# Target attention over 2048 histories: another order of scores and placing on TensorE, normalisation on GpSimd, weights and targets turned on the host, another warm-up and drain

## The chip, the cores and the metric

The kernel runs on one core of a Trainium2 chip. The time is in device microseconds, from the start of the program to its end. Engines: PE is TensorE (PEld its loading of weights), DVE is VectorE, ACT is ScalarE, POOL is GpSimd, SP is SyncE, which here only issues transfers (SPq in the profile's rows).

## The reference

For each of 2048 targets there is a history of 200 rows of 128 numbers. Scores of four heads of 32 are masked, go through a softmax, and weigh the values. All is float32.

```
q = (target_item @ W_q).reshape(b, H, HD)               # b 2048, H 4, HD 32
k = (history_sequence @ W_k).reshape(b, S, H, HD)       # S 200, D 128
v = (history_sequence @ W_v).reshape(b, S, H, HD)
scores = jnp.einsum('bhd,bshd->bhs', q, k) / SCALE
scores = jnp.where(mask[:, None, :] == 0, NEG, scores)
attn = jax.nn.softmax(scores, axis=-1)
out = jnp.einsum('bhs,bshd->bhd', attn, v).reshape(b, A)
return out @ W_o
```

The kernel never forms k and v. It multiplies W_q with W_k per head beforehand, gives each target a vector per head in the space of the history (u), and scores the raw history with it; the weighted sum of the raw history then goes through the product of W_v and W_o.

## The kernel before, in words

The 2048 targets are done in 64 pairs (`NP`) of two groups of 16; three pairs are a round (`RING` 3, `ROUND` 96 targets). A pair's history is 3.3 MB. SyncE loads it in four quarters: half 0 (12 of 25 rows a partition) of both groups, the next pair's mask, then half 1 (13 rows) of both groups. There are buffers for three pairs (`hist`), and the load of a half waits until the matmuls of `context` of three pairs before have read that half (`ctx_done`).

The work of a pair p, by what it needs:

- VectorE turns the history in blocks of 32x32 (`turn(p, i, half)`, four instructions, L468), since the scores need the feature on the partitions.
- `scores(p, ring, i)` on TensorE (L263): 32 matmuls per group.
- `maximum` on VectorE (L477) adds the mask's bias and takes the max; `exponent` on ScalarE (L392) writes `probs` and their sum.
- `turn_probs` on VectorE: reciprocal of the sum (L486), normalisation `weights = probs * inv_sum` (L488), block turn (L492).
- `place(q)` on TensorE (L277) spreads the probabilities over partitions into `ps_p`; `expand(p)` on ScalarE (L401) writes them with eight instructions into the zero pattern `p_pad`.
- `context(ring, half)` on TensorE (L294): 200 small matmuls of `p_pad` with the raw history.
- `finish` (ACT, L410), `turn_context` (PE, L304), `copy_context` (ACT, L416); once a round `outputs` (PE, L311) and `store` (ACT, L424).

GpSimd prepares `u_pad` from the vectors u (`spread`, L206, 16 small copies a pair, two pairs ahead) and the bias from the mask (`mask_bias`, L210). Once a round TensorE turns the next targets (`transpose_target`, L247) and makes the next u (`combine`, L252), which ScalarE copies (`copy_combined`, L387).

Each engine runs a list in program order, written out by hand, and waits on semaphores. TensorE's list is `step(q, ring, r)`: it places pair q, turns the contexts of pair q-1, does the target turn, the combination or the outputs where the ring says so, then the scores of pair q+1, then the contexts of pair q. Steps 0 and 1 and the last two are unrolled; the others run in a loop of three. VectorE's list interleaves pairs:

```
turn(p, 0, 0); maximum(p-1); turn(p, 1, 0); turn_probs(p-1); turn(p, 0, 1); turn(p, 1, 1)
```

ScalarE's list for pair q is `exponent(q)`, `finish(q-1)`, `expand(q)`, `copy_context(q-1)`, then `copy_target`, `copy_combined` or `store` where the round has one. So an exponential stands behind the expansion and the copies of the pair before.

At the start TensorE turns the three weights and the first targets, makes the products of the weights, and runs 68 transpositions of the identity (`IDLE_TURNS`, L358) before the first scores.

## Time and profile before

| | |
|---|---|
| median of 3 runs | 597.23 us (596.51 to 601.8) |
| the profiled execution | 596.54 us, with a span of 594.7 us in its trace |
| busy share of the span | PE 93%, PEld 75%, DVE 88%, ACT 45%, POOL 52% |
| transfers | 217.58 MB read, 1.05 MB written, mean 369 GB/s |
| TensorE's granted clock over the span | 0.984 of full speed |

The shares are means over a fill, an even part and a drain, which differ much. TensorE is busy nearly always, and so is VectorE; which of them, or which transfer, sets the time must be read from single steps. The page's chain of what ended last lies 81% on PE, 8% on ACT and 4% on DVE.

### The profile page before, as it was taken

How to read it: one execution, taken by the hardware profiler on the slowest of the kernel's cores; microseconds unless marked ns; L12 is line 12 of the kernel's file. 1: busy time of each engine (PE TensorE's matmuls, PEld its weight loads, DVE VectorE, ACT ScalarE, POOL GpSimd, SP SyncE). 2: the span in 40 equal slices, each digit the busy share in tenths (PEclk: the TensorE clock that was granted, in tenths of full speed). 3: DMA queues.
4: the chain of work that ended last, by engine and by line, in shares of the span. 5: the costliest groups of instructions: out<-in, count | busy, mean ns of one | idle time of the engine just before them, and what ended most of it. 6: DMA issues, size and time to landing. Idle time of an engine off the chain costs nothing.

```text
span 594.7 us, 41652 instructions
## 1 busy us (share of the span) xinstructions
PE 551.6 (93%) x18637; PEld 444.7 (75%) x18637; DVE 520.8 (88%) x577; ACT 265.9 (45%) x909; POOL 306.3 (52%) x1123
## 2 busy tenths in 40 slices
PE   5789789999999999999999999999999999999985
PEld 4666567787777878787787877878787777877865
DVE  4576778999999999999999999999999999999960
ACT  2033334554455445544554455445544554455532
POOL 6535353644637465383744737456383654737300
PEclk9978999999999999999999999999999999999998
DMA  8957879999999999999999999999999999999930
GB/s 314 398 178 249 282 279 406 399 400 403 404 408 399 406 406 404 401 402 404 402 406 402 406 401 402 407 400 409 403 403 402 410 398 402 401 406 401 398 134 7
DMA packets 49807, 219.17 MB, mean 369 GB/s; under 512 B 5888, under 2 KB 16656, under 8 KB 49760
## 3 DMA queue, kind: packets, MB, share of 16 engines
q1 hardware_dynamic: 49056, 217.60, 92.9%
q0 software_dynamic: 704, 1.05, 0.5%
q8 instruction: 16, 0.26, 0.2%
q14 instruction: 31, 0.25, 0.1%
HBM read 217.58 MB, written 1.05 MB: 368 GB/s over the span
## 4 chain that ended last, share of the span: by engine, by line
PE 81%; ACT 8%; issue 5%; DVE 4%; DMA 1%; SPq 1%; POOLq 0%; POOL 0%; DVEq 0%
PE ps_c L294 30%; PE ps_s L263 28%; PE ps_p L277 11%; ACT p_pad L401 8%; PE ps_y L304 4%; PE ps_u L252 3%; PE ps_u L311 3%; DVE blocks L468 3%; PE ps_p L358 2%; DMA w_in<-L_rec_W_o 1%; DVE probs_t L492 1%; DVE weights L488 1%; SPq L149 0%; SPq L158 0%; SPq L143 0%
## 5 line engine op out<-in xcount | busy, mean ns | idle before, releaser
L468 DVE STREAM_TRANSPOSE blocks<-hist 128x1536 f32<-128x1536 f32 (+1 forms) x256 | 455.7, 1814 | 9.0 <-DMA hist<-r_history_sequence 8.7
L206 POOL COPY u_pad<-u_sb 32x32 f32<-32x32 f32 x1024 | 234.2, 229 | 196.2 <-ACT u_sb L387 138.2
L263 PE MATMUL ps_s<-blocks,u_pad 128*32 128x200 f32 x4096 | 198.9, 342 | 14.8 <-ACT p_pad L401 9.7
L294 PE MATMUL ps_c<-hist,p_pad 64*32 64x128 f32 x12800 | 202.2, 272 | 8.7 <-issue 6.5
L294 PEld LDWEIGHTS ps_c<-hist,p_pad 64*32 64x32 f32 x12800 | 183.5, 106 | 30.5 <-issue 28.2
L401 ACT ACTIVATE p_pad<-ps_p,own 128x200 f32<-128x200 f32 x512 | 170.2, 444 | 42.9 <-PE ps_p L277 42.9
L263 PEld LDWEIGHTS ps_s<-blocks,u_pad 128*32 128x32 f32 x4096 | 125.7, 111 | 71.8 <-DVE blocks L468 25.6
L410 ACT COPY ctx_sb<-ps_c 128x128 f32<-128x128 f32 x128 | 27.8, 269 | 139.7 <-PE ps_c L294 139.7
L210 POOL TENSOR_SCALAR bias<-mask 128x200 f32<-128x200 int32 x64 | 56.4, 882 | 61.2 <-DVE neg_max L477 56.7
L392 ACT ACTIVATE probs<-neg_score,neg_max 128x200 f32<-128x200 f32 x64 | 29.6, 463 | 125.9 <-DVE neg_max L477 125.9
L277 PE MATMUL ps_p<-probs_t,place_sel 128*64 128x112 f32 x1024 | 64.0, 267 | 7.9 <-DVE probs_t L492 5.4
L277 PEld LDWEIGHTS ps_p<-probs_t,place_sel 128*64 128x64 f32 x1024 | 50.2, 138 | 24.6 <-DVE probs_t L492 16.5
L477 DVE CUSTOM_DVE_ANT_0 neg_score<-ps_s,bias 128x200 f32<-128x200 f32 x64 | 23.5, 367 | 37.2 <-PE ps_s L263 37.0
L304 PE MATMUL ps_y<-par_sel,ctx_sb 128*128 128x64 f32 x256 | 42.6, 289 | 0.0
L304 PEld LDWEIGHTS ps_y<-par_sel,ctx_sb 128*128 128x128 f32 x256 | 33.8, 192 | 9.2 <-issue 0.3
L492 DVE STREAM_TRANSPOSE probs_t<-weights 128x224 f32<-128x224 f32 x64 | 26.3, 411 | 2.8 <-DVE weights L488 0.2
L416 ACT COPY ctx_t<-ps_y 128x128 f32<-128x128 f32 x64 | 28.0, 437 | 0.1
L252 PE MATMUL ps_u<-x_t,w_qk 128*128 128x96 f32 x176 | 24.8, 286 | 0.9 <-ACT w_qk L430 0.9
L311 PE MATMUL ps_u<-w_vo,ctx_t 128*96 128x128 f32 x176 | 23.5, 277 | 0.5 <-ACT ctx_t L416 0.5
L488 DVE TENSOR_SCALAR weights<-probs,inv_sum 128x200 f32<-128x200 f32 x64 | 21.5, 336 | 2.3
L252 PEld LDWEIGHTS ps_u<-x_t,w_qk 128*128 128x128 f32 x176 | 22.2, 198 | 1.3 <-ACT w_qk L430 1.1
L311 PEld LDWEIGHTS ps_u<-w_vo,ctx_t 128*96 128x96 f32 x176 | 19.9, 163 | 0.8 <-ACT ctx_t L416 0.6
(42 smaller groups left out, 110.4 us busy)
## 6 DMA issues: line engine op xcount, KB each, us to landing
hist<-r_history_sequence SPq DMA_DIRECT2D x128, 832.0 KB, 8.1
hist<-r_history_sequence SPq DMA_DIRECT2D x128, 768.0 KB, 5.8
mask<-r_mask SPq DMA_DIRECT2D x64, 100.0 KB, 6.0
x_sb<-r_target_item SPq DMA_DIRECT2D x21, 48.0 KB, 8.5
out<-out_sb POOLq DMA_DIRECT2D x21, 48.0 KB, 4.7
w_in<-L_rec_W_q SPq DMA_DIRECT2D x1, 64.0 KB, 1.9
w_in<-L_rec_W_k SPq DMA_DIRECT2D x1, 64.0 KB, 2.0
w_in<-L_rec_W_v SPq DMA_DIRECT2D x1, 64.0 KB, 4.5
```

The costliest lines, as they stand in the source:

```text
L206: pool.tensor_copy(to, source[Q * c:Q * c + Q, a]).then_inc(u_pad_ready, 1)
L210: pool.tensor_scalar(bias[p % 2][:, :], mask_sb[p % RING][:, :], 0.0, BIG, ALU.is_equal, ALU.mult).then_inc(bias_ready, 1)
L252: mm = pe.matmul(ps_u[:, h * ROUND:(h + 1) * ROUND], w_qk[:, h, :], x_t[:, :], start=True, stop=True)
L263: mm = pe.matmul(ps_s[ring][Q * b:Q * b + Q, 0:S].rearrange("p (t j) -> p t j", j=J), u_pad[ring][:, i, b, c, :], blocks[slot][:, :, c, J ...
L277: mm = pe.matmul(ps_p[64 * alpha:64 * alpha + 64, 0:4 * TQ * 16].rearrange("p (q x i r) -> p x q i r", q=TQ, x=4, i=2)[:, x], place_sel[:, ...
L294: mm = pe.matmul(ps_c[alpha][at:at + Q, 0:D], p_pad[ring][rows, t + par, i, :], hist[2 * ring + i][rows, t + par, :], start=(t == 0), stop ...
L304: mm = pe.matmul(ps_y[:, 64 * alpha:64 * alpha + 64], ctx_sb[:, alpha, :], par_sel[:, :, :].rearrange("p i r -> p (i r)"), start=True, sto ...
L311: mm = pe.matmul(ps_u[0:ROUND, H * ROUND:H * ROUND + D], ctx_t[:, h, :], w_vo[:, h, :], start=(h == 0), stop=(h == H - 1))
L392: act.activation(probs[p % 2][:, :], neg_score[p % 2][:, :], ACT.Exp, bias=neg_max[:, 0:1], scale=-1.0, accum_out=row_sum[p % 2][:, 0:1]). ...
L401: op = act.activation(p_pad[p % RING][:, :, :, H * k:H * k + H].rearrange("p t i h -> p (t i) h"), source[:, k // 4], ACT.Copy, scale=own[ ...
L468: dve.transpose(blocks[g % BLOCKS][:, t0:t1].rearrange("p t c k -> p (t c k)"), hist[g % SLOTS][:, t0:t1, :].rearrange("p t d -> p (t d)") ...
L492: dve.transpose(probs_t[:, :, :].rearrange("p q r -> p (q r)"), weights[:, :]).then_inc(probs_turned, 1)
```

## The change

What it does, part by part:

- TensorE's `step` begins with half of the scores of pair q+1, then places pair q, then does the other half; then the turn of the contexts and the combination or the outputs; then it waits for the expansion and does one transposition of the identity, then the contexts.
- VectorE no longer normalises. It makes the reciprocal after its second turn, then does a third turn, then turns the probabilities. GpSimd normalises (`normalise`), ahead of the spreading of the pair two further on.
- `p_pad` is one buffer instead of three.
- Weights W_q, W_k, W_v and the targets come transposed from the host, ahead of the launch. The turns on TensorE, their copies on ScalarE, and the loads of targets once a round go; the rest of the targets comes in one transfer of 1 MB behind pair 1's history. ScalarE issues four of the small loads at the start.
- The warm-up is 50 matmuls of 32 columns. One step is unrolled ahead of the loop instead of two; two steps are unrolled behind it, and the last is written out, with 12 transpositions ahead of its contexts and the outputs between the two halves. `outputs` also runs in the first round, on zeros.

The core of the diff:

```diff
@@ pool @@
+            def normalise(p):
+                pool.wait_ge(inv_ready, p + 1)
+                wait(pool, probs_turned, p)
+                pool.tensor_scalar(weights[:, 0:S], probs[p % 2][:, :], inv_sum[:, 0:1], None,
+                                   ALU.mult).then_inc(weighted, 1)
...
             for p in range(NP):
+                pool.wait_ge(bias_ready, min(p + 2, NP))
+                normalise(p)
+                pool.wait_ge(weighted, p + 1)
                 if p + 2 < NP:
-                    pool.wait_ge(bias_ready, p + 2)
                     spread(p + 2)
@@ tensor @@
-            def step(q, ring, r, first=False, ahead=True, targets=True):
+            def step(q, ring, r, first=False):
 
+                scores(q + 1, (ring + 1) % RING, 0)
                 place(q)
+                scores(q + 1, (ring + 1) % RING, 1)
                 if not first:
                     pe.wait_ge(ctx_copied, 2 * q)
                     turn_context()
-                if targets and (ring == 2 or first):
-                    transpose_target(r + 2 if ring == 2 else 1)
-                if targets and ring == 0 and not first:
-                    combine(r + 1)
-                if ring == 1 and not (isinstance(r, int) and r == 0):
-                    outputs(q - 1)
-                if ahead:
-                    scores(q + 1, (ring + 1) % RING, 0)
-                    pe.wait_ge(expanded, q + 1)
-                    scores(q + 1, (ring + 1) % RING, 1)
-                else:
-                    pe.wait_ge(expanded, q + 1)
+                    if ring == 0:
+                        combine(r + 1)
+                    if ring == 1:
+                        outputs(q - 1)
+
+                pe.wait_ge(expanded, q + 1)
+                pe.transpose(ps_p[:, 0:P], ident[:, :], ident[:, :])
                 context(ring, 0)
                 context(ring, 1)
                 if first:
+                    pe.wait_ge(rest_loaded, 16)
+                    pe.wait_ge(x_zero, 1)
                     combine(1)
...
-            for _ in range(IDLE_TURNS):
-                pe.transpose(ps_p[:, 0:P], ident[:, :], ident[:, :])
-            for i in range(2):
-                scores(0, 0, i)
+            for _ in range(IDLE):
+                pe.matmul(ps_p[0:Q, 0:Q], ident[:, 0:Q], ident[:, 0:Q], start=True, stop=True)
+            scores(0, 0, 0)
+            scores(0, 0, 1)
             step(0, 0, 0, first=True)
-            step(1, 1, 0)
             with pe.Fori(0, LOOPS) as r:
+                step(3 * r + 1, 1, r)
                 step(3 * r + 2, 2, r)
                 step(3 * r + 3, 0, r + 1)
-                step(3 * r + 4, 1, r + 1)
-            step(NP - 2, 2, NR - 2, targets=False)
-            step(NP - 1, 0, NR - 1, ahead=False, targets=False)
+            step(NP - 3, 1, NR - 2)
+            step(NP - 2, 2, NR - 2)
+
+            place(NP - 1)
+            pe.wait_ge(ctx_copied, 2 * (NP - 1))
+            turn_context()
+            for _ in range(WARM):
+                pe.transpose(ps_s[1][:, 0:P], ident[:, :], ident[:, :])
+            pe.wait_ge(expanded, NP)
+            context(0, 0)
             outputs(NP - 1)
+            context(0, 1)
@@ scalar @@
-                wait(act, ctx_done, 2 * (p - RING) + 2)
+                wait(act, ctx_done, 2 * p)
...
+            store(NR - 2)
             finish(NP - 1)
-            store(NR - 2)
@@ vector @@
+            def reciprocal(p):
                 dve.wait_ge(exp_done, p + 1)
-                if p == 0:
-                    dve.wait_ge(weights_zero, 1)
-                wait(dve, probs_turned, p)
+                wait(dve, weighted, p)
                 dve.reciprocal(inv_sum[:, :], row_sum[p % 2][:, :]).then_inc(inv_ready, 1)
-                dve.wait_ge(inv_ready, p + 1)
-                dve.tensor_scalar(weights[:, 0:S], probs[p % 2][:, :], inv_sum[:, 0:1], None,
-                                  ALU.mult).then_inc(weighted, 1)
```

How it moves the instructions. On TensorE, in the loop, the step with the outputs (`scores` L263, `place` L277, `turn_context` L304, `outputs` L311, `context` L294), before:

```order
L273 REGISTER_ALU
L277 MATMUL ps_p<-probs_t,place_sel 64x7x16 x8
L319 REGISTER_ALU
L304 MATMUL ps_y<-par_sel,ctx_sb 128x64 x2
L311 MATMUL ps_u<-w_vo,ctx_t 96x128 x4
L257 ISA
L259 ISA
L263 MATMUL ps_s<-blocks,u_pad 32x200 x16
```

And after (the same functions now stand at L256, L270, L297, L304 and L287; L322 is the transposition):

```order
L256 MATMUL ps_s<-blocks,u_pad 32x200 x16
L130 REGISTER_ALU
L270 MATMUL ps_p<-probs_t,place_sel 64x7x16 x8
L250 REGISTER_ALU
L256 MATMUL ps_s<-blocks,u_pad 32x200 x16
L314 REGISTER_ALU
L297 MATMUL ps_y<-par_sel,ctx_sb 128x64 x2
L304 MATMUL ps_u<-w_vo,ctx_t 96x128 x4
L322 MATMUL ps_p<-ident 128x128
L287 MATMUL ps_c<-hist,p_pad 32x128 x100
```

Half of the scores moved ahead of the placing; both halves moved ahead of the context's turn and the outputs, which now stand between the scores and the contexts.

On VectorE, one pair in the even part, from the max on (`turn` L468, reciprocal L486, normalisation L488, turn of the probabilities L492), before:

```order
L477 ISA neg_score,neg_max<-ps_s,bias 128x200
L477 ISA neg_max 128x1
L468 STREAM_TRANSPOSE blocks<-hist 128x1536
L486 RECIPROCAL inv_sum<-row_sum 128x1
L488 TENSOR_SCALAR weights<-probs,inv_sum 128x200
L492 STREAM_TRANSPOSE probs_t<-weights 128x224
L468 STREAM_TRANSPOSE blocks<-hist 128x1664 x2
```

And after (now L467, L458, L474 and L479):

```order
L467 ISA neg_score,neg_max<-ps_s,bias 128x200
L467 ISA neg_max 128x1
L458 STREAM_TRANSPOSE blocks<-hist 128x1536
L474 RECIPROCAL inv_sum<-row_sum 128x1
L458 STREAM_TRANSPOSE blocks<-hist 128x1664
L479 STREAM_TRANSPOSE probs_t<-weights 128x224
L458 STREAM_TRANSPOSE blocks<-hist 128x1664
```

The third block turn moved between the reciprocal and the turn of the probabilities, and the normalisation left the engine.

On SyncE, the first transfers, before (`w_in` weights, `x_sb` and `x_t` targets):

```order
L143 DMA w_in<-L_rec_W_q 128x128
L143 DMA w_in<-L_rec_W_k 128x128
L144 DMA x_sb<-r_target_item 96x128
L158 DMA hist<-r_history_sequence 128x1536 x2
L149 DMA mask<-r_mask 128x1x200 x2
L167 DMA w_in<-L_rec_W_v 128x128
```

And after, as far as the transfer of the remaining targets:

```order
L137 DMA w_in<-L_rec_W_q 128x128
L151 DMA hist<-r_history_sequence 128x1536 x2
L142 DMA mask<-r_mask 128x1x200 x2
L151 DMA hist<-r_history_sequence 128x1664 x2
L151 DMA hist<-r_history_sequence 128x1536 x2
L142 DMA mask<-r_mask 128x1x200
L151 DMA hist<-r_history_sequence 128x1664 x2
L159 DMA x_t<-r_target_item 128x1952
```

The history moved ahead of all but one of the small loads, and the remaining targets stand ahead of pair 2's history.

## Rows read from the trace of the kernel before

**Rows 1.** Windows, even part: span; busy us (count) by engine; clock, DMA share, GB/s.

```profile
92.80:575.20 482.40, 468.48 (x16521) 378.68 (x16516) 461.06 (x513) 232.75 (x797) 260.39 (x955) 1.00 1.00 399
```

**Rows 2.** Timeline of a step: start us, us, engine, line, operation, count, idle before.

```profile
304.32 2.84 PEld L294 LDWEIGHTS ps_c<-hist,p_pad 64*32 64x32 f32 x200 [0.32 <-issue]
...
305.96 0.80 SPq L158 DMA_DIRECT2D hist<-r_history_sequence  x2
...
307.44 0.99 PE L277 MATMUL ps_p<-probs_t,place_sel 128*64 128x112 f32 x16
...
308.35 0.66 PE L304 MATMUL ps_y<-par_sel,ctx_sb 128*128 128x64 f32 x4
308.47 2.66 ACT L401 ACTIVATE p_pad<-ps_p,own 128x200 f32<-128x200 f32 x8 [0.57 <-PE ps_p L277]
...
308.85 1.07 PE L311 MATMUL ps_u<-w_vo,ctx_t 128*96 128x128 f32 x8
...
309.84 2.98 PE L263 MATMUL ps_s<-blocks,u_pad 128*32 128x200 f32 x64
310.97 0.43 ACT L416 COPY ctx_t<-ps_y 128x128 f32<-128x128 f32 x1
311.13 0.36 ACT L424 COPY out_sb<-ps_u 96x128 f32<-96x128 f32 x1
311.25 1.18 PEld L263 LDWEIGHTS ps_s<-blocks,u_pad 128*32 128x32 f32 x32 [0.24 <-DVE blocks L468]
...
312.88 0.37 DVE L477 CUSTOM_DVE_ANT_0 neg_score<-ps_s,bias 128x200 f32<-128x200 f32 x1 [0.26 <-PE ps_s L263]
...
313.29 0.46 ACT L392 ACTIVATE probs<-neg_score,neg_max 128x200 f32<-128x200 f32 x1 [1.80 <-DVE neg_max L477]
...
314.87 0.12 DVE L486 RECIPROCAL inv_sum<-row_sum 128x1 f32<-128x1 f32 x1
...
315.03 0.33 DVE L488 TENSOR_SCALAR weights<-probs,inv_sum 128x200 f32<-128x200 f32 x1
```

**Rows 3.** Timeline: ScalarE's copy of the combination, in the step with `combine`.

```profile
302.70 0.59 ACT L387 COPY u_sb<-ps_u 128x384 f32<-128x384 f32 x1
```

**Rows 4.** Single loads issued at 94.3, 102.7, 104.2, 305.96, 9.83: us to landing last.

```profile
hist<-r_history_sequence SPq DMA_DIRECT2D x1, 768.0 KB, 4.1
...
hist<-r_history_sequence SPq DMA_DIRECT2D x1, 768.0 KB, 4.3
...
hist<-r_history_sequence SPq DMA_DIRECT2D x1, 832.0 KB, 7.1
...
hist<-r_history_sequence SPq DMA_DIRECT2D x1, 768.0 KB, 4.6
...
hist<-r_history_sequence SPq DMA_DIRECT2D x1, 768.0 KB, 15.9
```

**Rows 5.** Groups by line and form, whole span: busy us, mean ns, idle before.

```profile
L468 DVE STREAM_TRANSPOSE blocks<-hist 128x1664 f32<-128x1664 f32 x128 | 234.6, 1870 | 1.6 <-DMA hist<-r_history_sequence 1.6
...
L210 POOL TENSOR_SCALAR bias<-mask 128x200 f32<-128x200 int32 x64 | 56.4, 882 | 61.2 <-DVE neg_max L477 56.7 <-PE ps_s L263 1.0
```

**Rows 6.** Timeline: the max of pairs 0, 2 and 6.

```profile
24.82 0.37 DVE L477 CUSTOM_DVE_ANT_0 neg_score<-ps_s,bias 128x200 f32<-128x200 f32 x1 [7.09 <-PE ps_s L263]
...
48.02 0.37 DVE L477 CUSTOM_DVE_ANT_0 neg_score<-ps_s,bias 128x200 f32<-128x200 f32 x1 [2.51 <-PE ps_s L263]
...
92.77 0.37 DVE L477 CUSTOM_DVE_ANT_0 neg_score<-ps_s,bias 128x200 f32<-128x200 f32 x1 [0.79 <-PE ps_s L263]
```

**Rows 7.** Windows of the warm-up alone: PE and PEld busy (count), clock, DMA, GB/s.

```profile
12.30:16.30 4.00, 4.00 (x19) 4.00 (x20) 1.00 1.02 399
16.50:21.70 5.20, 5.20 (x50) 5.17 (x48) 1.00 1.02 414
```

**Rows 8.** Timeline of the drain: contexts of pair 62 (end) and pair 63.

```profile
578.93 0.64 PE L294 MATMUL ps_c<-hist,p_pad 64*32 64x128 f32 x17 [1.06 <-issue]
...
583.24 4.64 PE L294 MATMUL ps_c<-hist,p_pad 64*32 64x128 f32 x200 [2.17 <-ACT p_pad L401]
```

105 lines of the change are left out of this document (43 added, 62 removed).

## The prediction

> **What bounds the kernel now.** I read the windows by stage first, then the timeline of one step, then the loads. The window from 92.8 us, where the max of pair 6 stands [rows 6], to 575.2 is even running with the array's clock at 1.00 [rows 1]; ahead of it lies the fill, behind it the drain. It holds 513 instructions of VectorE, nine a step, so 57 steps: 482.4 / 57 = 8.46 us each. What one step costs decides nearly everything, since 0.1 us of it is 5.7 us.
>
> Within a step TensorE is full. Counted from the start of the placing matmuls at 307.44 [rows 2]: placing 0.91, the turn of the contexts 0.50, the outputs 0.99, the first half of the scores 1.41, the second 1.50, the contexts 3.12 (304.32 to 307.44). These add up to 8.43. VectorE is nearly full as well: its wait before the max is 0.26 us. ScalarE is not: it expands the probabilities from 308.47, copies the outputs, and then waits 1.80 us for the max before the exponential [rows 2]. The transfers run at 399 GB/s with their engines busy all the time [rows 1], yet no block turn waits for one in the even part: a load that is issued 1.64 us into the contexts (305.96 against 304.32) lands 4.6 us later, and other such loads 4.1 to 4.3 [rows 4], just before its turn.
>
> **The even part.** Four edits meet here.
>
> VectorE loses the normalisation, 0.36 us with its gap, the 0.33 us row of 315.03. GpSimd takes it. Nothing shows this form there. The nearest row is the mask's operation on the same 128x200, 0.88 us [rows 5]; its floor is VectorE's 0.33. I take 0.88, as it is the same engine. The cover is a block turn of 1.87 us [rows 5], so 0.88 and two handovers are hidden; with that cover gone it would cost 1.0 us a step. On GpSimd the spreading and the mask wait behind it. In the even part GpSimd is busy 260.39 / 57 = 4.6 us a step [rows 1], so there is room for 0.88 more. VectorE's saving is worth nothing unless VectorE ends last.
>
> TensorE loses one target turn in three steps and gains one small transposition in each. The transpositions of the warm-up took 5.2 us for 50 at the full clock, 0.10 us each [rows 7]. In the order after, a step is 1.41 + 0.91 + 1.50 + 0.50 + 0.99 + 0.10 + 3.12 = 8.53 us where there are outputs or a combination (two steps in three). In the third, the expansion ends last: it starts 1.03 us after placing, lasts 2.66, and 0.12 passes until TensorE starts, so 3.81 + 0.10 + 3.12 + 1.41 = 8.44. The mean is 8.50: TensorE's own order gains nothing, because it was full before. What the moved order does remove is the wait of the scores' second half for the expansion.
>
> The moved order costs ScalarE its slack. Before, from placing to the end of the scores there were 5.31 us, which hid the expansion and two copies. Now there are 0.91 + 1.50 = 2.41, so the slack of 1.80 turns into a delay of 1.1 us. In the step with outputs these end 3.90 us after placing starts; the copy of the context starts at 4.00, the store at 4.16 and lasts 0.36, the exponential starts at 4.52, and the reciprocal 0.61 later at 5.13 (0.46 for the exponential, an estimate of 0.15 for reading its sum and the handover), the block turn at 5.29 and ends at 7.16; half the scores start at 7.21 and the next placing 1.41 later, at 8.62. With the copy of 0.59 us [rows 3] for the combination it is 8.69. With 8.44 for the third step the mean is **8.58 us**.
>
> The loads then decide. The contexts, which free the history buffers, no longer follow the scores at once: they start 0.91 + 1.50 + 0.50 + 0.99 + 0.10 = 4.00 us after placing (3.91 in the third step), though the turns on VectorE keep their place against the max. Taking 3.97, the first quarter of the pair three further on is issued at 5.61 and lands at 9.91, 4.3 us later. The third quarter lands 4.3 us behind it (issues at 102.70 and 104.19, landing after 4.3 and 7.1 us [rows 4]), at 14.21. Its turn takes 1.87, the handover 0.05, half the scores 1.41: 17.54 us to a placing that is two steps on, so 8.77 a step. With the shortest latency, 4.1 us [rows 4], it is 8.67. The stream itself sets no such limit: 414 GB/s in [rows 7] would allow 8.2 us for a pair's 3.4 MB. I take **8.73**, nearer to 8.77 because the quiet 4.1 came once, right after a stall. Against 8.46 that is +0.27 x 57 = **+15.4 us**. The bounds are 8.44 and 8.85, which are -1 and +22 us.
>
> The page "DMA: Bandwidth & Descriptors" of the Trainium skill, in "Anatomy of one DMA", gives 2.0 us and the bytes over 436 GB/s for a transfer from GpSimd's queue, which as an estimate is 3.8 us for a quarter. The trace has 4.3 for SyncE's queue, and the trace decides. By the page the loads would chain at about 8.5 us, and the engines' 8.58 would rule, which is the first rival.
>
> **The fill.** The weights and targets come turned from the host, so two turns with their copies go, and the weights for the output are no longer loaded behind the history. The warm-up of 68 transpositions, 12.3 to 21.7 us [rows 7], becomes 50 matmuls of 32 columns, at most 5 us by the 0.10 of a full transposition. Then the loads decide. VectorE had done the turns that stand ahead of the first max at 24.82 - 7.09 = 17.7 [rows 6]. SyncE now issues two small loads fewer ahead of the history, at 0.4 us each (0.80 for two in [rows 2]), so these turns end at 16.9, and with them stands the first max, instead of at 24.82. The next max must let the first turn of pair 2 pass, whose load, issued at 9.83, landed 15.9 us later at 25.7 [rows 4]. It is 0.8 earlier, but the rest of the targets, now 1 MB in one transfer ahead of it, costs 2.4 us at 414 GB/s. So turn at 27.3 for 1.8, and max 1 at 29.1. The combination behind the first contexts still holds the second exponential; I add 1.2 to a step of 8.7 for it: max 2 at 39.0 against 48.02, 9 us ahead.
>
> From there to max 6 the kernel before took 44.75 us for four steps whose code runs for the first time, 11.2 us a step, with gaps like the first of [rows 8]. After, the loop is entered one step earlier, so one such step becomes even: 11.7 + 11.7 + 9.7 + 8.7 = 41.8, and max 6 stands at 80.8 against 92.77: **-11.9 us**. The two full cold steps are taken at a little over the mean of 11.2, the two others below it, since the last of the four was already half even. Bounds: -6, if small matmuls don't raise the clock, and -15.
>
> **The drain.** Two unrolled steps follow the loop and then a part of a third, so one more cold step: +1.1, the idle time ahead of the first of [rows 8]. The contexts of pair 62 start 1.5 us later. The last contexts ran at half clock, 4.64 us [rows 8]; with the transpositions ahead of them 3.12 are possible, -1.5. The outputs go between the two halves, +0.9, and the store ahead no longer holds the last, -0.5. The sum is **+1.5**, bounds 0 and +4.
>
> The page "TensorE: Matmul & The Clock Gate" of the Trainium skill says in "PE-mode transpose" that transpositions don't count as activity for the clock. Here they do: 19 records in the first 4.0 us and then 50 in 5.2 [rows 7]. By the page the -1.5 would go, and the time would be 1.5 us longer, which is within the range.
>
> **The sum.** 594.7 + 15.4 - 11.9 + 1.5 = 599.7 us of span. The profiled execution took 596.54 with a span of 594.7, so 1.84 lie around it, and it stands 0.7 below the median of 597.23. That gives 601.5, or 602.2 against the median; I say **602**.
>
> **Rivals.** *The loads land in time.* Latency falls below 4.1 us once the stream is no longer full, and the engines' 8.58 decides: +7 instead of +15, 593 us. For it: 4.1 was seen. Against it: both latencies were taken where the queue had drained. Chance 0.2.
>
> *The step stays or shrinks.* Then the fill alone shows. The contexts are entered with 0.32 us idle on TensorE's loads [rows 2]; if the small transposition swallows that, and ScalarE's copies overlap more than I count, the step is 8.40 to 8.46, and the time 583 to 587. Against it: the chain over the exponential has no such idle time in it. Chance 0.15.
>
> *The loads chain worse (slower than before).* After a disturbance the first quarter took 4.6 us [rows 4] and the queue caught up only slowly. Now each late landing delays two steps on, and nothing catches up. At 8.83 the time is 608; it passes +1% (603.2) from 8.75 us a step. Speaking for it: the sum by the usual 4.3 is already 8.77. Chance 0.3.
>
> *It doesn't hide the normalisation.* GpSimd takes far longer than 0.88, above 1.6 us, and each step gains the difference. The spreading copies run beside the same turns without lengthening them, so I give it 0.03, 610 us and more.
>
> **How the numbers follow.** The forecast, 8.66 to 8.75 a step with its fill, has 0.32. A step of 0.1 us either way is 6 us and the fill may be off by 4, so within each case some chance passes the 1% bounds, 591.3 and 603.2; 1% is about what a measurement of this kernel can tell from no change. Faster: 0.15, half of the first rival's 0.2, and 0.02 of the forecast, 0.27. Slower: most of the 0.3, the 0.03 and 0.05 of the forecast, 0.34. Same: 0.39. The range 583 to 611 leaves out 0.05 below and 0.08 above.
>
> **What the next profile should show.** The distance of two maxes in the even part, 8.6 to 8.8 us; idle time of the reciprocal on VectorE, ended by ScalarE's exponential; block turns that wait for history loads, in many steps; ScalarE without its wait for the max; transfers at some 390 GB/s; first max near 17, the seventh near 81. I am wrong if the turns never wait for loads and the step is under 8.5, or if the fill ends where it did.

## The result, and the profile after

The changed kernel takes 624.08 us (median of 4 runs, 622.41 to 627.03), the kernel before 597.11 beside it: a ratio of 1.044, 95% interval 1.040 to 1.048. It is slower, by more than the range of 583 to 611 allowed. The profiled execution has a span of 623.4 us.

The profile's page of the changed kernel, its line of busy time and three of its groups (busy us, mean ns, then the idle time just before them and what ended it):

```profile
PE 557.1 (89%) x18727; PEld 444.7 (71%) x18727; DVE 504.5 (81%) x513; ACT 260.6 (42%) x885; POOL 357.1 (57%) x1189
...
L458 DVE STREAM_TRANSPOSE blocks<-hist 128x1536 f32<-128x1536 f32 (+1 forms) x256 | 469.7, 1836 | 70.1 <-DMA hist<-r_history_sequence 68.9
...
L206 POOL TENSOR_SCALAR weights<-probs,inv_sum 128x200 f32<-128x200 f32 x64 | 50.7, 791 | 179.2 <-issue 169.8
...
L387 ACT ACTIVATE probs<-neg_score,neg_max 128x200 f32<-128x200 f32 x64 | 30.6, 479 | 8.0 <-DVE neg_max L467 8.0
```

VectorE's block turns now wait 68.9 us in all for the history. Between 100 and 550 us alone they wait 47.4 us in 82 times; in the kernel before it was 0.5 us in 3 times. GpSimd's normalising takes 0.79 us, a little under the 0.88 taken for it. ScalarE, which waited 1.80 us a step for the max [rows 2], waits for it once in the whole run, 8.0 us at the start: its slack is gone, as forecast.

The windows of the changed kernel, from the max of pair 6 to 0.7 us before that of pair 63, and the fill before (us, busy time with the number of instructions of PE, PEld, DVE, ACT, POOL, granted clock, DMA share, GB/s):

```profile
85.70:602.20 516.50, 478.84 (x16541) 383.70 (x16545) 446.94 (x455) 228.19 (x778) 309.54 (x1029) 1.00 0.96 371
...
18.16:85.70 67.54, 53.02 (x1534) 39.96 (x1535) 47.19 (x49) 21.93 (x74) 33.65 (x114) 0.90 0.84 311
```

From max to max the 57 steps take 602.88 - 85.70 = 517.2 us instead of the 482.4 of [rows 1], and the transfers run at 371 instead of 399 GB/s: they wait too. TensorE is busy for 93% of this stretch, 97% before; VectorE for 87%, 96% before. Four maxes, from the timeline of VectorE (start, us): of pairs 2, 6, 62 and 63.

```profile
42.84 0.37 DVE L467 CUSTOM_DVE_ANT_0 neg_score<-ps_s,bias 128x200 f32<-128x200 f32 x1 [2.00 <-PE ps_s L256]
...
85.70 0.37 DVE L467 CUSTOM_DVE_ANT_0 neg_score<-ps_s,bias 128x200 f32<-128x200 f32 x1 [0.25 <-POOL bias L200]
...
590.78 0.33 DVE L467 CUSTOM_DVE_ANT_0 neg_score<-ps_s,bias 128x200 f32<-128x200 f32 x1
...
602.88 0.37 DVE L467 CUSTOM_DVE_ANT_0 neg_score<-ps_s,bias 128x200 f32<-128x200 f32 x1 [4.56 <-PE ps_s L256]
```

Fifty-six even steps in 590.78 - 85.70 = 505.08 us are **9.02 us** each; before, the same 56 took 566.85 - 92.77 = 474.08 us, 8.47 each. The last step is 12.1 instead of 8.3. The bill, against 594.7: the 56 even steps +31.0; the last, cold step +3.8; pair 6 at 85.70 instead of 92.77, -7.1; the drain behind the last max 20.5 instead of 19.5, +1.0; the sum is 623.4, the span that was found.

Now one round of the chain of the loads, from the changed kernel's timeline (start, us, engine, what, and the idle time before it): placing, contexts, the issue of the load, the turns that wait for it, the scores, the next placings.

```profile
298.60 0.99 PE L270 MATMUL ps_p<-probs_t,place_sel 128*64 128x112 f32 x16
...
302.61 3.10 PE L287 MATMUL ps_c<-hist,p_pad 64*32 64x128 f32 x200
...
304.25 0.80 SPq L151 DMA_DIRECT2D hist<-r_history_sequence  x2
...
307.42 0.99 PE L270 MATMUL ps_p<-probs_t,place_sel 128*64 128x112 f32 x16
...
308.67 1.78 DVE L458 STREAM_TRANSPOSE blocks<-hist 128x1536 f32<-128x1536 f32 x1 [0.71 <-DMA hist<-r_history_sequence]
...
311.44 3.10 PE L287 MATMUL ps_c<-hist,p_pad 64*32 64x128 f32 x200
...
312.87 1.91 DVE L458 STREAM_TRANSPOSE blocks<-hist 128x1664 f32<-128x1664 f32 x1 [0.30 <-DMA hist<-r_history_sequence]
...
314.92 1.56 PE L256 MATMUL ps_s<-blocks,u_pad 128*32 128x200 f32 x32 [0.37 <-DVE blocks L458]
...
316.41 0.99 PE L270 MATMUL ps_p<-probs_t,place_sel 128*64 128x112 f32 x16
317.73 1.78 DVE L458 STREAM_TRANSPOSE blocks<-hist 128x1536 f32<-128x1536 f32 x1 [0.86 <-DMA hist<-r_history_sequence]
...
321.94 1.91 DVE L458 STREAM_TRANSPOSE blocks<-hist 128x1664 f32<-128x1664 f32 x1 [0.32 <-DMA hist<-r_history_sequence]
...
323.99 1.56 PE L256 MATMUL ps_s<-blocks,u_pad 128*32 128x200 f32 x32 [0.47 <-DVE blocks L458]
325.48 0.99 PE L270 MATMUL ps_p<-probs_t,place_sel 128*64 128x112 f32 x16
```

From 298.60 to 316.41 two steps pass: 4.01 to the contexts, 1.64 to the issue, 4.42 until the quarter has landed and its turn starts, 4.20 to the third quarter's turn, 2.05 to the scores, 1.49 to the placing: 17.81. From 307.42 to 325.48 it is 18.06, with 4.65 for the landing. The forecast had 17.54 with the same links. In 40 such rounds between 100 and 550 us, the landing took 4.1 to 5.5 us, 4.5 in the mean.

The same chain was there before, but with room in it. The load issued at 305.96 landed after 4.6 us [rows 4], at 310.56; its turn is the last of the three that the timeline of the kernel before counts together here, and began near 310.9:

```profile
307.30 5.32 DVE L468 STREAM_TRANSPOSE blocks<-hist 128x1664 f32<-128x1664 f32 x3
```

The contexts then started 0.1 us ahead of the max (312.75 against 312.88). Now they start 1.0 to 1.2 us behind it (302.61, 311.44 and 320.42 against 301.37, 310.37 and 319.43), and the 0.3 us of room are gone.

In one place the profile misleads. It puts 27 waits of the scores between 100 and 550 us, 15.0 us in all, down to GpSimd's `u_pad`. But the copies that go on then are for a pair further on. The scores start 0.14 us behind the end of the third turn in the three rounds from 303.88 on, so it is the turn that they wait for.

### The profile page after: what moved, and what is told of

It is laid out like the page before. It is cut to its first block, busy times and chain, and to the rows that moved or that the text cites. A ratio compares the mean times of both kernels' runs of the same rounds, so it can differ in the third digit from the quotient of the medians.

```text
span 623.4 us, 41775 instructions
## 1 busy us (share of the span) xinstructions
PE 557.1 (89%) x18727; PEld 444.7 (71%) x18727; DVE 504.5 (81%) x513; ACT 260.6 (42%) x885; POOL 357.1 (57%) x1189
## 4 chain that ended last, share of the span: by engine, by line
PE 49%; issue 23%; POOL 14%; DMA 7%; ACT 3%; DVE 3%; SPq 1%; POOLq 0%; DVEq 0%; ACTq 0%
PE ps_s L256 26%; PE ps_c L287 10%; PE ps_p L270 8%; POOL u_pad L196 8%; DMA hist<-r_history_sequence 7%; POOL weights L206 5%; ACT p_pad L396 3%; DVE blocks L458 2%; PE ps_u L304 2%; PE ps_y L297 2%; PE ps_u L244 1%; SPq L151 1%; PE ps_p L322 1%; DVE neg_score L467 1%; POOL bias L200 0%
## 5 line engine op out<-in xcount | busy, mean ns | idle before, releaser
L458 DVE STREAM_TRANSPOSE blocks<-hist 128x1536 f32<-128x1536 f32 (+1 forms) x256 | 469.7, 1836 | 70.1 <-DMA hist<-r_history_sequence 68.9
L256 PE MATMUL ps_s<-blocks,u_pad 128*32 128x200 f32 x4096 | 204.0, 340 | 32.0 <-POOL u_pad L196 18.3
L287 PE MATMUL ps_c<-hist,p_pad 64*32 64x128 f32 x12800 | 202.0, 271 | 7.7 <-issue 6.8
L287 PEld LDWEIGHTS ps_c<-hist,p_pad 64*32 64x32 f32 x12800 | 182.7, 105 | 17.9 <-issue 8.8
L256 PEld LDWEIGHTS ps_s<-blocks,u_pad 128*32 128x32 f32 x4096 | 123.9, 111 | 88.0 <-POOL u_pad L196 42.1
L206 POOL TENSOR_SCALAR weights<-probs,inv_sum 128x200 f32<-128x200 f32 x64 | 50.7, 791 | 179.2 <-issue 169.8
L270 PEld LDWEIGHTS ps_p<-probs_t,place_sel 128*64 128x64 f32 x1024 | 51.4, 140 | 21.2 <-issue 21.2
L270 PE MATMUL ps_p<-probs_t,place_sel 128*64 128x112 f32 x1024 | 65.4, 272 | 0.0
L297 PEld LDWEIGHTS ps_y<-par_sel,ctx_sb 128*128 128x128 f32 x256 | 33.4, 190 | 20.7 <-issue 19.7
L297 PE MATMUL ps_y<-par_sel,ctx_sb 128*128 128x64 f32 x256 | 42.1, 287 | 0.5 <-ACT ctx_sb L405 0.5
L467 DVE CUSTOM_DVE_ANT_0 neg_score<-ps_s,bias 128x200 f32<-128x200 f32 x64 | 21.8, 341 | 15.4 <-PE ps_s L256 14.3
L322 PE MATMUL ps_p<-ident 128*128 128x128 f32 x63 | 18.4, 292 | 15.2 <-ACT p_pad L396 15.2
L244 PE MATMUL ps_u<-x_t,w_qk 128*128 (+1 forms) x176 | 24.8, 286 | 2.5 <-DMA x_t<-r_target_item 2.5
L304 PE MATMUL ps_u<-w_vo,ctx_t 128*96 128x128 f32 x184 | 24.6, 277 | 0.5 <-ACT ctx_t L411 0.5
L479 DVE STREAM_TRANSPOSE probs_t<-weights 128x224 f32<-128x224 f32 x64 | 23.7, 370 | 1.0 <-POOL weights L206 1.0
```

The lines of the kernel that those rows point to most:

```text
L206: pool.tensor_scalar(weights[:, 0:S], probs[p % 2][:, :], inv_sum[:, 0:1], None, ALU.mult).then_inc(weighted, 1)
L244: mm = pe.matmul(ps_u[:, h * ROUND:(h + 1) * ROUND], w_qk[:, h, :], x_t[:, bass.ds(at, ROUND)] if not isinstance(r, int) else x_t[:, at:at ...
L256: mm = pe.matmul(ps_s[ring][Q * b:Q * b + Q, 0:S].rearrange("p (t j) -> p t j", j=J), u_pad[ring][:, i, b, c, :], blocks[slot][:, :, c, J ...
L270: mm = pe.matmul(ps_p[64 * alpha:64 * alpha + 64, 0:4 * TQ * 16].rearrange("p (q x i r) -> p x q i r", q=TQ, x=4, i=2)[:, x], place_sel[:, ...
L287: mm = pe.matmul(ps_c[alpha][at:at + Q, 0:D], p_pad[rows, t + par, i, :], hist[2 * ring + i][rows, t + par, :], start=(t == 0), stop=(t + ...
L297: mm = pe.matmul(ps_y[:, 64 * alpha:64 * alpha + 64], ctx_sb[:, alpha, :], par_sel[:, :, :].rearrange("p i r -> p (i r)"), start=True, sto ...
```

## The experiments

"Even step" is the distance of the maxes of pairs 9 and 60, by 51; the kernel before has 8.47 by it, the changed one 9.02. Ratios are to the kernel before, timed beside.

| run | us | ratio, 95% interval | even step |
|---|---|---|---|
| e1_step_order_back | 665.53 | 1.114 (1.108 to 1.120) | 9.74 |
| e2_step_order_alone | 649.71 | 1.086 (1.081 to 1.090) | 9.30 |
| e3_gpsimd_normalises_alone | 671.89 | 1.122 (1.117 to 1.127) | 9.77 |
| e4_short_loads | 596.08 | single run | 8.65 |
| e5_fill_and_drain_alone | 593.00 | 0.991 (0.987 to 0.995) | 8.46 |
| e6_before_short_loads | 592.87 | single run | 8.48 |
| e7_step_order_alone_short_loads | 639.62 | single run | 9.25 |
| e8_placing_first | 622.07 | 1.039 (1.030 to 1.048) | 9.00 |
| e9_two_unrolled_steps | 754.89 | single run | long stalls |
| e10_exponential_before_copy | 747.56 | 1.249 (1.243 to 1.256) | long stalls |
| e11_no_normalising | 626.59 | single run | 9.04 |
| e12_no_holding_transpositions | 626.50 | single run | 9.03 |
| e13_one_unrolled_exponential_first | 591.84 | 0.989 (0.984 to 0.994) | 8.54 |
| e14_two_unrolled_shifted | 913.25 | single run | long stalls |
| e15_two_unrolled_shifted_exponential_first | 898.60 | 1.502 (1.495 to 1.510) | long stalls |
| e16_changed_exponential_first | 624.57 | single run | 9.00 |
| e17_two_unrolled_back | 591.25 | 0.986 (0.982 to 0.991) | 8.47 |
| e18_changed_shifted | 772.42 | single run | long stalls |

### The two edits of the even step, each alone

**e1**: the changed kernel, TensorE's order as before.

```diff
-                scores(q + 1, (ring + 1) % RING, 0)
                 place(q)
-                scores(q + 1, (ring + 1) % RING, 1)
 ...
+                scores(q + 1, (ring + 1) % RING, 0)
                 pe.wait_ge(expanded, q + 1)
-                pe.transpose(ps_p[:, 0:P], ident[:, :], ident[:, :])
+                scores(q + 1, (ring + 1) % RING, 1)
```

> The changed kernel with TensorE's order of a step as before (placing, turn of contexts, combination or outputs, both halves of the scores with the wait for the expansion between them, contexts, no small transposition); all else stays changed: GpSimd normalises behind the third block turn, new fill and drain. Theory A (late contexts free the history buffers late, and the loads chain over two steps): contexts follow the scores again, the loads are back in time, the even step falls from 9.02 to 8.40-8.45 us, and with the fill's gain the time is 587-592 us. Rival B (the third block turn and GpSimd's normalisation lengthen the way to the placing): the step stays at 8.8-9.1, 610-625 us. Rival C (the stream of loads is slower whatever the order, some 375 GB/s): the same 615-625 us.

All three theories failed: 665.5 us, slower than the whole change. Rival B had the cause, a longer way to the placing, but not its size. The timeline of TensorE and VectorE in a step of e1:

```profile
303.66 1.89 DVE L456 STREAM_TRANSPOSE blocks<-hist 128x1664 f32<-128x1664 f32 x1
...
305.47 0.37 DVE L477 STREAM_TRANSPOSE probs_t<-weights 128x224 f32<-128x224 f32 x1
...
305.98 0.99 PE L270 MATMUL ps_p<-probs_t,place_sel 128*64 128x112 f32 x16 [1.38 <-DVE probs_t L477]
...
311.42 0.37 DVE L465 CUSTOM_DVE_ANT_0 neg_score<-ps_s,bias 128x200 f32<-128x200 f32 x1 [2.04 <-PE ps_s L256]
```

The probabilities' turn now stands behind the third block turn, and the old order of TensorE places first of all. So TensorE stands for 1.38 us at the placing, and VectorE then stands 2.04 for the scores. The turns hardly wait for loads: between 100 and 550 us, 4.3 us in 11 times.

**e2**: the kernel before with TensorE's new order alone. **e3**: the kernel before with GpSimd's normalising and the third turn ahead of the probabilities' turn alone.

> The kernel before with the new order of a step on TensorE alone (half the scores, placing, the other half, turn of contexts, target turn, combination or outputs, wait for the expansion, one small transposition, contexts). VectorE normalises as before, three p_pad buffers, old fill and drain. Theory A: the even step is 8.9-9.1 us as in the changed kernel, the time 624-634 us. Rival B: without GpSimd's normalisation the step is 8.5-8.65 us, 600-608 us.

> The kernel before with GpSimd's normalisation behind the third block turn alone; TensorE's order, fill and drain as before. Theory A: TensorE was full at 8.43 us a step and still is, so the step is 8.40-8.50 and the time 594-600 us. Placing moves 1.8 us against the max, so a gain is possible only where VectorE ended last. Rival B: the later placing makes the expansion late, the step grows to 9 us, 620-630 us.

e2, with 649.7 us and 9.30 a step, came out above both of its cases. e3, with 671.9, is far from the 594 to 600 of its theory and above its rival's 620 to 630 too: its even step is that of e1 (9.77 and 9.74), with the same kind of wait, 1.29 us at a placing. So neither edit is good by itself. +8.6% and +12.2% alone, they are +4.4% together: the new order puts half of the scores, which needs the third turn, ahead of the placing, and GpSimd's normalising lets the third turn come first.

### What the loads cost

**e4** is the changed kernel with short loads, **e6** the kernel before with them, **e7** is e2 with them. From pair 3 on each load brings only 6 of its 12 or 13 rows a partition:

```diff
+                        t9 = t1 if p < RING else t0 + 6
-                            hist[g % SLOTS][:, t0:t1, :], history_v[g * P:(g + 1) * P, t0:t1, :],
+                            hist[g % SLOTS][:, t0:t9, :], history_v[g * P:(g + 1) * P, t0:t9, :],
```

> The changed kernel, but from pair 3 on every load of history brings only 6 of the 12 or 13 rows a partition (old rows stay in the buffers, so the output differs from the reference's); all waits on the buffers stay. Theory A: a load lands about 1 us earlier and the third quarter 3 us earlier, so the loads stop binding and the engines' own chain shows, 8.6-8.75 us a step, 600-607 us. Rival B (GpSimd or ScalarE set the step): unchanged at 9.02, 622-626 us.

> The kernel before, with each load from pair 3 on cut to 6 rows of its half (the rest of the slot keeps old data, so the output is not the reference's); VectorE, TensorE and all waits stay. Control for the short loads of the changed kernel. Theory A (before, the loads are not what ends a step): even step within 0.05 of 8.46 us, 594 to 598. Rival B (short loads speed up any version, by less traffic): even step 8.2 us or less, under 585.

> TensorE's new step order alone (the 650 us run) with each load from pair 3 on cut to 6 rows, so not the reference's output. Theory A (late contexts bind this version through the loads, and VectorE's normalising ahead of the third turn adds its 0.9 us only in that chain): even step 8.6 to 8.8, 605 to 620. Rival B (the normalising itself sets the step, since the first half of the scores waits for the third turn): even step 9.1 or more, 635 or more.

The list of waits, of e4 and then of e7 (us in total, times, longest):

```profile
DVE neg_score L468 <- PE ps_s L257: 34.3, 60, 3.8
DVE inv_sum L475 <- ACT probs L388: 22.0, 42, 4.6
DVE blocks L459 <- DMA hist<-r_history_sequence: 16.3, 26, 4.3
```

```profile
DVE neg_score L478 <- PE ps_s L264: 59.1, 64, 8.0
...
DVE inv_sum L487 <- ACT probs L393: 21.9, 42, 4.4
...
DVE blocks L469 <- DMA hist<-r_history_sequence: 7.7, 6, 5.2
```

Before, short loads leave the even step as it was (8.48 against 8.47): the loads bound nothing in it. (Its 592.9 us are below the 594 of its theory, by a shorter fill: pair 6 at 87.83.) In the changed kernel they take it from 9.02 to 8.65. So of the 0.55 us lost a step the loads hold 0.37, and the engines' own chain 0.18; in e4 the reciprocal waits for ScalarE's exponential in 42 of the steps, and the max for the scores, as the forecast had it. The time, 596.1 us, is below the 600 of its theory, since the fill became shorter too (pair 6 at 79.05). e7 met its rival: with the loads out of the way the new order alone still takes 9.25, so there it is VectorE's normalising and the probabilities' turn, 0.9 us ahead of the third turn, that count. From 9.25 (e7) to 8.65 (e4), GpSimd's edit is worth some 0.6 us a step under the new order with short loads; with full loads, where they bind, it is 0.28 (9.30 in e2 to 9.02). Both pairs of kernels differ in fill, drain and `p_pad` as well; e5 below, which has these and the old even step, takes 8.46.

**e8** places ahead of both halves of the scores in the changed kernel.

> The changed kernel with placing moved ahead of the first half of the next scores, nothing else. Theory A (late contexts bind through the loads; placing comes 0.9 us and the contexts some 0.5 us sooner): no wait for loads over 0.3 us, even step 8.6 to 8.8, 600 to 612. Rival B (TensorE now stands still at the placing until the probabilities are turned, which VectorE does behind its third block turn, and the half of the scores that covered this comes later): even step 9.1 to 9.6, 630 to 655.

It is 622 us, no better and no worse than the changed kernel, between its two theories. From the timeline of TensorE in e8:

```profile
306.12 3.10 PE L287 MATMUL ps_c<-hist,p_pad 64*32 64x128 f32 x200
310.67 0.99 PE L270 MATMUL ps_p<-probs_t,place_sel 128*64 128x112 f32 x16 [1.44 <-DVE probs_t L479]
```

TensorE waits 1.44 us here for the probabilities' turn, 54 us in all, and the turns still wait 64 us for loads, against 69. The placing moved ahead of the half of the scores, but it now waits for that turn, so it hardly came sooner.

**e11** leaves GpSimd's normalising out and keeps its waits and signals.

> The changed kernel with GpSimd's normalising (0.79 us each) shortened to the write of one unused number, with all its waits and signals; the weights stay zero, so the output is not the reference's. Theory A (GpSimd's work lies beside the third turn and no chain of the step runs over it; loads and TensorE's order set 9.02 us): even step 8.95 to 9.02, 619 to 624. Rival B (GpSimd's 0.8 us or its share of VectorE's access stands in the step's chain): even step 8.7 or less, under 608.

An even step of 9.04, a little above its theory's 9.02: the 0.79 us on GpSimd is hidden. That rival is out. The third turn takes 1.91 us here as well, so it isn't GpSimd's normalising that lengthens it from the 1.87 of [rows 5].

### The drain and the fill

**e12**: `WARM = 12` becomes 0.

> The changed kernel without the 12 transpositions of the drain. Theory A (they keep TensorE's clock up over its wait for the last expansion): the granted clock falls after the last placing and the last two context halves and outputs (4.9 us of work) take 2 to 4 us more, drain 22.5 to 24.5 us. Rival B (the clock would have stayed up, and 1.48 us of transpositions lay in a wait of 2.3 us anyway): drain 20.5 us within 0.3.

The end of e12, TensorE's timeline and two windows (columns as above):

```profile
610.51 0.66 PE L297 MATMUL ps_y<-par_sel,ctx_sb 128*128 128x64 f32 x4
613.33 1.59 PE L287 MATMUL ps_c<-hist,p_pad 64*32 64x128 f32 x96 [2.17 <-ACT p_pad L396]
```

```profile
610.00:615.00 5.00, 2.83 (x114) 2.35 (x110) 0.00 (x0) 3.06 (x10) 0.00 (x0) 1.00 0.02 3
615.00:620.00 5.00, 3.76 (x117) 2.94 (x118) 0.00 (x0) 1.07 (x4) 0.54 (x1) 1.00 0.05 13
```

After 2.17 us of idle time, without any transposition, the clock is still 1.00 and the 96 records take the same 1.59 us. From the last max to the end it is 20.4 us, with the transpositions 20.5. The transpositions changed nothing here. In the kernel before the last contexts came behind the same 2.17 us of wait, yet they took 4.64 us [rows 8], and from 583.24 to 586.00 us the granted clock was 0.50. What sets this difference, no run shows.

**e5** keeps the fill, the drain and the turned weights, and undoes both edits of the even step; **e13** adds to it this edit of ScalarE's list, and **e16** makes the same edit in the changed kernel:

```diff
                 exponent(q)
+                r = q // RING
+                if q % RING == 1 and r + 1 < NR:
+                    copy_combined(r + 1)
 ...
-                if q % RING == 0 and r + 1 < NR:
-                    copy_combined(r + 1)
```

> The changed kernel with both steady edits undone: TensorE's steps in the order of the kernel before (placing, contexts' turn, outputs, first half of the next scores, second half, contexts), VectorE normalising ahead of the third block turn. What is left of the change is the fill, the drain and the weights and targets handed over transposed. Theory A (both steady edits are the loss, the fill is worth what it showed): even step 8.46 us as before, pair 6's maximum at 82 to 86 us, drain 0.5 to 1.5 us longer; 587 to 592 us. Rival B (an earlier start only uses up loads that are then missing, and the even step pays it back): 595 to 599.

> The 593 us version (fill and drain of the change, steady steps as before, one unrolled step ahead of the loop) with ScalarE's copy of the next round's combined queries behind the next pair's exponential. Theory A (the copy held pair 1's exponential, and so its placing, in the fill; the loop keeps its place in the code and has no long stalls): pair 2's maximum at 38 to 40.5 us instead of 42.56, even step 8.46, no TensorE stall over 0.4 us in the loop, 588 to 592 us. Rival B (loads or cold steps take the gain back by pair 6): pair 6 within 0.5 us of 85.90, 592 to 594.

> The changed kernel with ScalarE's copy of the combined queries behind the next pair's exponential, nothing else. Tests the term of the fill. Theory A (pair 2's maximum came at 42.84 instead of the forecast 39.0 since pair 1's exponential stood behind that copy until 34.5, and GpSimd's spread of pair 2 behind its normalising): pair 2's maximum at 36.5 to 39.5, even step unchanged within 0.06 of 9.02, 618 to 623. Rival B (the half-speed clock and cold code set it): pair 2's maximum later than 41.5.

e5's theory holds for the steps: pair 6 at 85.90, then 8.46 a step, last step 10.8 (8.3 before), span 589.6. Its median of 593.0 is 1.0 above the range, and 0.5 to 1.4% faster than the kernel before. So the fill keeps its gain, and nearly all of the loss is in the even step. Now the fill of the changed kernel, timelines of ScalarE, VectorE and TensorE:

```profile
34.14 0.48 ACT L382 COPY u_sb<-ps_u 128x384 f32<-128x384 f32 x1 [4.51 <-PE ps_u L244]
34.52 0.46 ACT L387 ACTIVATE probs<-neg_score,neg_max 128x200 f32<-128x200 f32 x1
```

```profile
35.10 0.16 DVE L474 RECIPROCAL inv_sum<-row_sum 128x1 f32<-128x1 f32 x1 [4.17 <-ACT probs L387]
35.18 1.91 DVE L458 STREAM_TRANSPOSE blocks<-hist 128x1664 f32<-128x1664 f32 x1
```

```profile
37.23 2.30 PE L256 MATMUL ps_s<-blocks,u_pad 128*32 128x200 f32 x32 [3.13 <-DVE blocks L458]
39.46 1.76 PE L270 MATMUL ps_p<-probs_t,place_sel 128*64 128x112 f32 x16
```

The exponential of pair 1, whose max was ready at 29.2, stands behind the copy of the next round's vectors until 34.52. VectorE's list is in order, so the third turn of pair 2 waits behind the reciprocal of pair 1, which waits 4.17 us for that exponential, and TensorE stands 3.13 us for the turn. The half of the scores and the placing behind it run at a lower clock: 2.30 and 1.76 us instead of 1.56 and 0.99, with 0.73 granted from 37 to 39 us and 0.50 from 39 to 41.

With the copy behind the exponential (e16), pair 2's max comes at 39.39 instead of 42.84, as the forecast had it (39.0). But pair 6 stands at 86.58, no sooner, and the time stays at 624.6. The four steps between take it back: TensorE stands still with nothing to wait for 7.5 us in all instead of 4.6, in stalls of up to 2.4 us, and the turns wait 10.9 us for loads instead of 5.6. In e13 pair 2 gains only 0.6, far from its theory's 38 to 40.5, and pair 6 1.3.

How much of this hangs on the loads, e4 and e6 show. With short loads the four steps from pair 2 to pair 6 take 36.3 us instead of 42.9 in the changed kernel, and 38.8 instead of 44.8 in the kernel before. Some of that is turns that wait less for history; some is TensorE's stalls, 1.3 us instead of 4.6 in e4. Why these become shorter, no run separates.

### Where the loop lies in the code

**e9** is e5 with step 1 unrolled again ahead of the loop and one step fewer behind it; **e10** is e9 with ScalarE's edit.

```diff
+            step(1, 1, 0)
             with pe.Fori(0, LOOPS) as r:
-                step(3 * r + 1, 1, r)
                 step(3 * r + 2, 2, r)
                 step(3 * r + 3, 0, r + 1)
-            step(NP - 3, 1, NR - 2)
+                step(3 * r + 4, 1, r + 1)
             step(NP - 2, 2, NR - 2)
```

> The 593 us version (fill and drain of the change, steady steps as before) with step 1 unrolled again ahead of the loop and only one unrolled step behind it, so the layout of the kernel before: what 'one unrolled step' alone is worth. Theory A (the unrolled step is cold wherever it stands, so the change moved its stalls from the fill to the end): pair 6's maximum 1 to 2 us later than 85.90, the last step 2.5 us shorter (8.4 instead of 10.84), span 587.5 to 589.5. Rival B (a cold step costs more in the fill, where the half-speed clock stands in it too): pair 6 at 88.5 or later, span 590 to 593.

> The same as the run with two unrolled steps, and on ScalarE the copy of the combined queries of the next round moved behind the next pair's exponential. Theory A (in the fill, pair 1's exponential stood 5.2 us behind that copy, which waits for pair 0's contexts and the combination; placing of pair 1 then waits only for TensorE's own work): pair 2's maximum 1.5 to 2.5 us sooner than 42.56, all else equal, median 588 to 591, ratio to before 0.985 to 0.990. Rival B (TensorE's own row of contexts, combination, placing and cold scores sets pair 2's maximum, or loads do a pair later): pair 6 within 0.5 us of the run with two unrolled steps, 591 to 594.

No theory had 750 us. From TensorE's timeline in e9, and its row of the instruction queue (packets, MB, share), with that of the changed kernel behind it:

```profile
104.67 3.10 PE L279 MATMUL ps_c<-hist,p_pad 64*32 64x128 f32 x200
115.13 1.76 PE L262 MATMUL ps_p<-probs_t,place_sel 128*64 128x112 f32 x16 [7.35 <-issue]
```

```profile
q8 instruction: 98, 1.61, 0.9%
```

```profile
q8 instruction: 17, 0.28, 0.2%
```

TensorE stands for 7.35 us with nothing to wait for, at the loop's start, then 0.83 and 2.10 us in the same pass; and the instruction queue brings 98 packets of code of 16.4 KB, where the whole code is 17. So the loop of three steps is loaded again as it runs. Behind the long stall the granted clock is 0.50 from 115.1 to 117.0 us (placing in 1.76). Four runs tried whether this follows the place of the loop. Their only edit is the number of short matmuls in the warm-up: `IDLE` 64 instead of 50 in e9 and e10 (**e14**, **e15**), 32 in e10 (**e17**), 68 in the changed kernel (**e18**).

> The 755 us version (two unrolled steps ahead of the loop) with 64 instead of 50 short matmuls in the warm-up, which moves everything behind them 14 matmuls later in TensorE's code; nothing else differs. Theory A (the stalls of some 8 us at each pass of the loop are code that is loaded again, and whether it is depends on where the loop's first and last instructions lie in the code): no stalls over 0.5 us in the loop, instruction queue some 17 packets instead of 98, even step 8.46, 588 to 594. Rival B (it is the loop that begins with step 2 instead of step 1, wherever it lies): 750 to 760 again.

> The same shift and ScalarE's copy behind the exponential, two unrolled steps ahead of the loop. Theory A (as in the two runs beside it, their gains add): 586 to 590, and 1 to 2 us under the version with one unrolled step. Rival B (the loop's layout still costs its repeated loads): 740 to 760.

> Two unrolled steps ahead of the loop, ScalarE's copy behind the exponential, and 32 instead of 50 matmuls in the warm-up: everything behind moves 18 matmuls forward in TensorE's code. The even steps are those of the 593 us version. Theory A (repeated loads of code depend on where the loop lies; 14 matmuls backward made them 188 instead of 98, so 18 forward bring them down): some 17 packets in the instruction queue, even step 8.46, last step 8.4 to 8.6, 586 to 592 us. Rival B (two unrolled steps ahead of the loop are bad at any place): over 640 us.

> The changed kernel with 68 instead of 50 matmuls in the warm-up, nothing else: 1.7 us more of warm-up, and everything behind it 18 matmuls later in TensorE's code. Theory A (place in the code decides, in the changed kernel too): instruction queue 60 packets or more instead of 17, over 700 us. Rival B (the changed kernel's loop, which begins with step 1, is safe at any place): 17 packets, 623 to 627.

The rows of the instruction queue of e14, of e17 and of e18:

```profile
q8 instruction: 188, 3.08, 1.5%
```

```profile
q8 instruction: 17, 0.28, 0.2%
```

```profile
q8 instruction: 98, 1.61, 0.9%
```

e14 and e15 went the wrong way for their theories' times and for their rivals' alike, 913 and 899 us. It is a matter of place all the same: matmuls that stand ahead of the loop in TensorE's code are 238 in the changed kernel and e5 (17 packets), 256 in e18 (98), 366 in e17 (17), 384 in e9 (98), 398 in e14 (188). Some 1,090 matmuls in 280 KB are 0.257 KB each, as an estimate, so the two cases with 98 packets, 128 matmuls apart, differ by just two packets of 16.4 KB: the loop starts at the same offset in one. The long stalls fit the packets. e9 and e18 have nine stalls of over 5 us, one at every second pass of the loop's 20; e14 has 19, one at each jump back; and 81 and 171 packets beyond the 17 are nine for each of them. Eighteen matmuls of warm-up, 1.2 us of work, cost the changed kernel 148 us. Why one offset reloads and another doesn't is left open.

The page "Runtime: NRT & Kernel Launch" of the Trainium skill, in "Instruction fetch mechanics", gives TensorE 128 KiB of instruction memory, filled in blocks of 16 KiB; the size of a packet agrees. It also warns that a taken branch out of two blocks stops for a fetch. The changed kernel's loop, 434 matmuls or some 111 KB by the estimate above, jumps back at each of its passes without one: its 17 packets are the whole code.

e17 also tells what one unrolled step is worth. Its pair 6 stands at 89.49, its last step takes 8.3; in e13 it is 84.60 and 11.2. So the unrolled step costs 4.9 us ahead of the loop and 2.9 behind it, by one profile each and with the shorter warm-up counted in. In the medians, 591.25 and 591.84, no difference shows. The ratios of e5, e13 and e17, 0.991, 0.989 and 0.986, have intervals that overlap: which of the three is best isn't shown.

## Why the prediction was wrong

**The even step: mechanism right, size wrong.** The forecast named all that the profile shows: the contexts 4.0 us after placing, block turns that wait for loads in most steps, ScalarE without its wait, the normalising hidden on GpSimd. e4 confirms both layers, the engines' chain (8.58 forecast, 8.65 found) and the loads over it. The step that failed is the sum of the loads' chain, 17.54 us and "I take 8.73". Found were 17.81 and 18.06 in two rounds, and 9.02 a step. The landing took 4.42 and 4.65 instead of 4.3 (4.5 in the mean of 40 rounds), the third turn 1.91 instead of 1.87, the handover 0.14 instead of 0.05, the half of the scores with its switch to placing 1.49 instead of 1.41, the contexts' start 4.01 instead of 3.97; only the distance of the third quarter was shorter, 4.20 instead of 4.3. Each is small, and nearly all have one sign. On top of that the 8.77 of the sum was taken down to 8.73 for a 4.1 us load seen once, though [rows 4] had a 4.6 as well. From 8.73 to 9.02 over 56 steps is 16 us, two thirds of the miss of 23.7 in the span. The rival "loads chain worse" had the mechanism and the side, but stopped at 8.83. The page "DMA: Bandwidth & Descriptors" of the Trainium skill, in "Anatomy of one DMA", gives 3.8 us for a landing, as an estimate. With it the miss would have been larger; the trace, with 4.42 and 4.65, disagrees.

**The fill.** -11.9 forecast, -7.1 found. Pair 0 came at 18.2 (16.9), pair 1 at 28.9 (29.1), pair 2 at 42.8 (39.0), pair 6 at 85.7 (80.8). Of the 4.9 us that are missing at pair 6, 3.8 are missing at pair 2 already. "I add 1.2" for the exponential behind the copy was too little, as the third turn and half of the scores hung on it as well, and TensorE then ran at a lower clock. But e16 shows that this alone is not what set pair 6: put right, it gave 39.4 and 86.6. The second failing term is the four steps behind it: 41.8 forecast, 42.9 found in the changed kernel, 47.2 in e16. They were taken as the price of code that runs for the first time. With short loads they take 36.3 (e4), so most of what they cost beyond even steps hangs on the loads too. By which way stays open.

**The last step and the drain.** "One more cold step: +1.1" was 3.8: a stall of 2.27 us and then scores and placing at a lower clock, with 0.77 granted over 595 to 600 us and 0.50 over its last 2 us.

```profile
596.63 0.66 PE L287 MATMUL ps_c<-hist,p_pad 64*32 64x128 f32 x23 [2.27 <-issue]
597.22 2.49 PE L256 MATMUL ps_s<-blocks,u_pad 128*32 128x200 f32 x32
599.64 1.68 PE L270 MATMUL ps_p<-probs_t,place_sel 128*64 128x112 f32 x16
```

With the 1.0 behind the last max that is +4.8 in all against +1.5, over its bound of +4. The -1.5 for the last contexts was taken too large, and its reason was wrong. They took 4.0 us in two parts instead of 4.57, at a granted clock of 1.00; and the transpositions held nothing, since without them the clock stayed at 1.00 (e12). Nor do the windows of [rows 7] show the clock rise during transpositions: the granted clock is 1.00 in both, though the transpositions became twice as fast.

**What was not forecast at all** is that the two edits of the even step belong together: alone each costs twice or nearly three times as much as the whole change (+8.6% and +12.2% against +4.4%). The working costed them only together.

## What to carry to other kernels

Where a wait closes on itself over several steps (contexts free a buffer, a load fills it, a turn, scores, placing, contexts), add its links at their usual length and not at their quickest, and compare it with the engines' own step: before this change that chain had some 0.3 us of room, and contexts that start 1.1 to 1.4 us later against the max turned it into the bound. Try such a thing with shortened loads on both kernels; it splits the step at once. And look at the packets of the instruction queue of every version of a long unrolled loop: more than the code's own number is a loop that loads itself again, and a few instructions ahead of it can make or break that.

## What was not expected of the hardware

- A loop of some 111 KB of TensorE's code (estimated from 280 KB for 1,090 matmuls) ran without loading any of it again at two places in the code (17 packets in all), and loaded 81 or 171 packets of 16.4 KB more at three others, nine for each long stall; 18 matmuls more ahead of it took the changed kernel from 624 to 772 us (e18, one run).
- In steps whose code ran for the first time TensorE stood still with nothing to wait for, up to 2.3 us at a time in the changed kernel. Behind the 2.27 us in its last step the granted clock was 0.50 (598 to 600 us), and scores and placing took 2.49 and 1.68 us instead of 1.56 and 0.99. With short loads the stalls of the fill were 1.3 us in all instead of 4.6 (e4).
- After a wait of 2.17 us with nothing to do TensorE's granted clock was still 1.00 (e12); after the same wait in the kernel before it was 0.50.
- VectorE's block turns of 128x1664 took 1.87 us each in the kernel before and 1.90 in the mean in the changed kernel. GpSimd's normalising isn't the reason: without it (e11) the mean is the same. What the reason is stays open.
